# Unread transposes of W0 ahead of W1's on TensorE, a second pair of PSUM banks for one block's M, and a mask written by VectorE

## What is computed

```python
x = x + einsum('bct,bcd->bdt', x, W0[itok_B_0_7])      # x: 128 x 64 x 512 fp32, W0: 8 x 64 x 64
x = x + einsum('bct,bcd->bdt', x, W1[itok_B_1_198])    # W1: 200 x 64 x 64
```

## Time and profile before

| | us |
|---|---|
| Median of 3 runs | 93.66 (93.46, 93.66, 95.83) |
| Time of the profiled execution | 94.32 |
| Its span, first to last instruction | 92.5 (92.54 with two decimals) |
| What lies around the span | 1.8 |
| Busy: TensorE 72.8, VectorE 60.9, ScalarE 50.6, GpSimd 23.8 | |

### The profile page before, as it was taken

How to read it: one execution, slowest core, us unless ns; L and a number is a source line. 1 busy time by engine, 2 the same in 40 slices (tenths; PEclk the granted TensorE clock), 3 DMA queues, 4 the chain that set the end, 5 groups by cost and what they waited for, 6 DMA issues and landing times.

```text
span 92.5 us, 2284 instructions
## 1 busy us (share of the span) xinstructions
PE 72.8 (79%) x836; PEld 38.7 (42%) x836; DVE 60.9 (66%) x115; ACT 50.6 (55%) x95; POOL 23.8 (26%) x124
## 2 busy tenths in 40 slices
PE   0400009999299999999999999999999999999700
PEld 0200008899154545435445544754444444444200
DVE  0086003389527887888778788878788788787740
ACT  2300001468626776777567677677576676676630
POOL 4220009989999989000000000000000000000000
PEclk9999999999999999999999999999999999999995
DMA  0999999999999999999999999999999999879695
GB/s 16 330 457 390 430 395 420 413 411 405 416 405 404 400 411 404 409 407 416 398 411 413 418 409 418 420 409 420 420 421 418 414 418 416 361 310 388 276 402 228
DMA packets 9180, 35.92 MB, mean 388 GB/s; under 512 B 721, under 2 KB 850, under 8 KB 9042
## 3 DMA queue, kind: packets, MB, share of 16 engines
q1 hardware_dynamic: 8880, 33.56, 90.4%
q0 software_dynamic: 144, 2.10, 5.4%
q10 hardware_dynamic: 146, 0.13, 0.5%
HBM read 19.01 MB, written 16.78 MB: 387 GB/s over the span
## 4 chain that ended last, share of the span: by engine, by line
PE 73%; DMA 13%; DVE 6%; issue 2%; DVEq 1%; ACT 1%; POOLq 0%; ACTq 0%
PE psum L225 61%; DMA w_rows<-in_L_cond_weights_dram,cond 10%; PE psum L206 7%; PE psum L187 6%; DVE w L244 5%; DMA cond<-in_itok_B_dram 3%; DVEq L64 1%; DVE xy L266 1%; ACT m_diag L258 1%; DVE w_rows L306 0%; POOLq L160 0%; ACTq L250 0%; POOLq L151 0%
## 5 line engine op out<-in xcount | busy, mean ns | idle before, releaser
L225 PE MATMUL psum<-xy,m_diag 64*128 64x512 f32 x256 | 56.6, 594 | 0.0
L266 DVE COPY xy<-psum 64x512 f32<-64x512 f32 x64 | 43.7, 684 | 12.7 <-PE psum L225 11.7
L266 ACT COPY xy<-psum 64x512 f32<-64x512 f32 x64 | 37.2, 581 | 19.1 <-PE psum L225 18.3
L225 PEld LDWEIGHTS psum<-xy,m_diag 64*128 64x128 f32 x256 | 24.4, 187 | 27.7 <-issue 27.1
L168 POOL COPY w0b<-w0t 64x64 f32 x112 | 21.6, 235 | 10.3 <-DMA w_rows<-in_L_cond_weights_dram,cond 8.5
L187 PE MATMUL psum<-ident,w_rows 128*64 128x128 f32 x64 | 9.5, 323 | 9.3 <-DVE w_rows L306 9.3
L244 ACT COPY w<-psum 64x256 f32<-64x256 f32 x16 | 5.8, 364 | 15.3 <-PE psum L187 14.5
L187 PEld LDWEIGHTS psum<-ident,w_rows 128*64 128x64 f32 x64 | 8.4, 158 | 10.7 <-DVE w_rows L306 9.8
L244 DVE COPY w<-psum 64x256 f32<-64x256 f32 x16 | 6.7, 417 | 3.4 <-PE psum L187 3.0
L206 PE MATMUL psum<-w,w0b 64*32 64x64 f32 x512 | 6.5, 224 | 1.8 <-ACT m_diag L258 0.9
L258 DVE TENSOR_SCALAR m_diag<-psum,mask 128x256 f32<-128x256 f32 (+2 forms) x14 | 6.7, 517 | 1.9 <-PE psum L206 1.7
(11 more groups left out here) (6 smaller groups left out, 0.8 us busy)
## 6 DMA issues: line engine op xcount, KB each, us to landing
xy<-in_x_dram SPq DMA_DIRECT2D x15, 1024.0 KB, 19.5
out_dram<-xy SPq DMA_DIRECT2D x15, 1024.0 KB, 11.1
xy<-in_x_dram SPq DMA_DIRECT2D x2, 512.0 KB, 7.4
out_dram<-xy SPq DMA_DIRECT2D x2, 512.0 KB, 3.4
w_rows<-in_L_cond_weights_dram ACTq DMA_DIRECT2D x1, 128.0 KB, 2.6
cond<-in_itok_B_dram SPq DMA_DIRECT2D x1, 0.5 KB, 2.4
subjects<-in_itok_B_dram ACTq DMA_DIRECT2D x1, 0.5 KB
w_rows<-in_L_cond_weights_dram,cond POOLq DMA_INDIRECT x1, 9.5
```

The costliest lines, as they stand in the source:

```text
L225: last = nc.tensor.matmul(psum[:, 2 * (s % Y_RING) + h, :], m_diag[rows, odd, v % M_RING, j, :], xy[rows, s, j * T:(j + 1) * T], start=j = ...
L266: copy(xy[rows, s, i * T:(i + 1) * T], psum[HALVES[i], 2 * (s % Y_RING) + h, :]).then_inc(done, 1)
```

## The change

Three edits:

1. Behind the 4 transposes of W0, TensorE issues 52 more (`WARM`) of the same tiles of W0. They write `psum` banks 0 to 5, nobody reads them, they wait for nothing and raise no semaphore; W1's transposes overwrite those banks later.
2. `M_BANK` becomes a list, `M_BANKS`: block 1's M goes to banks 4 and 5, all others' stay in 6 and 7. products(1) has therefore no wait for the copies of block 0's M any more (`if k >= 2`).
3. The mask is written by VectorE, 8 memsets of 32 x 1 at the head of its program, in place of 5 memsets on GpSimd; the gather no longer waits for it. The waits on `s_mask` in `copies` go from 4 to 8.

```diff
-    M_BANK = 6
+
+    M_BANKS = [6, 4, 6, 6, 6, 6, 6]
...
+    WARM = 52
...
-            nc.gpsimd.memset(mask[:, :], 0.0).then_inc(s_zeros, 1)
-            pool.wait_ge(s_zeros, 2)
-            for r, rows in enumerate(QUARTERS):
-                nc.gpsimd.memset(mask[rows, r % 2:r % 2 + 1], 1.0).then_inc(s_mask, 1)
-            pool.wait_ge(s_mask, SLOT)
...
             last.then_inc(s_w0_turned, 1)
+            for n in range(WARM):
+                nc.tensor.transpose(psum[0:C, n % W1_RING, 0:P], w0_rows[:, n % ROWS, :], ident[:, :])
...
-                if k >= 1:
+                if k >= 2:
+
                     pe.wait_ge(s_m_v, 2 * k)
                     pe.wait_ge(s_m_s, 2 * k)
...
-                                last = nc.tensor.matmul(psum[QUARTERS[r], M_BANK + odd, at:at + C],
+                                last = nc.tensor.matmul(psum[QUARTERS[r], M_BANKS[k] + odd, at:at + C],
...
-                      psum[:, M_BANK + odd, at:at + n * J * C].rearrange("q (w e i) -> q w i e", i=J, e=Q),
+                      psum[:, M_BANKS[k] + odd, at:at + n * J * C].rearrange("q (w e i) -> q w i e", i=J, e=Q),
...
-            eng.wait_ge(s_mask, SLOT)
+            eng.wait_ge(s_mask, 2 * SLOT)
...
+            for r, rows in enumerate(QUARTERS):
+                for b in range(2):
+                    nc.vector.memset(mask[rows, b:b + 1], 1.0 if b == r % 2 else 0.0).then_inc(s_mask, 1)
+
```

## The result

The changed kernel takes 98.28 us, median of 4 runs (96.92 to 98.7), against 93.8 for the kernel before: the ratio is 1.041, 95% interval 1.025 to 1.057. It is slower, where the prediction said 1.2% faster. Some executions of any of these kernels take some per cent longer than the others; the times given are medians of all runs, and the ratios are taken without those. The profiled execution took 98.11 us, with a span of 96.1 in place of 92.5.

A forecast was written before the change was run, and what follows sets the result against it. TensorE's chain and DMA were taken as bounds side by side, DMA slack only in the tail. Gains of 2.25 and 0.46 us make 2.7 on TensorE, of which 1.1 arrives: 93.66 - 1.1 = 92.5 us, range 91.2 to 93.7.

The forecast's parts named there:

- Nothing else waits for them: At the head: the 52 added transposes lie wholly beside the wait for W1's gather and hold up nothing.
- Is anything late next?: Check of x's loads, GpSimd's copies and the last products: none would hold up TensorE's apply starting 2.7 us earlier.
- The late rival: Head: the 52 transposes stay slow, end at 15.4 and start W1's transposes 1.5 us late; 94.8 us, chance 0.05.
- Of the 1.6 us of pause that is left I assume that it leaves the pace high.: Between the added transposes' end at 12.3 and W1's at 13.88: TensorE's idle spell does not cost the fast pace.
- The pause rival: Ahead of W1's transposes: 1.6 us idle loses the high pace, the banks alone gain 0.46 us; 93.2 us, chance 0.08.
- The 2.25 us themselves: W1's transposes run fast from the start, so ScalarE's copies end at 21.9 in place of 24.15: gain 2.25 us.
- Transposes alone bring the higher pace.: W1's transposes, from 13.88: nothing else runs before the pace changes, so transposes raise it, against the skill's rule.
- holds nothing before its first change: Granted clock column during W1's transposes: its early 1.00 is not a reading; the pace there is taken as 1.2 GHz.
- The banks, 0.46 us.: products(1) runs directly behind products(0), beside the copies of M0, so apply(0) starts 0.46 us earlier; bounds 0 and 0.46.
- The mask, worth 0 within 0.1 either way.: Head: the gather never waited for GpSimd's mask memsets, so moving them gains 0; bounds 0.1 us loss or gain.
- Two bounds, of 2.7 us won 1.1 arrives.: Tail: TensorE ends 2.7 us earlier, but the full line of stores lets 1.1 us through; 1.6 us is not seen.
- The estimate of 91.4 for the span: Whole kernel, profiled execution: span 92.5 less the 1.1 us gain makes 91.4.

The follow-up runs named there:

- e1: The kernel before with 26 small unread matmul calls (104 TensorE instructions) behind W0's transposes and nothing else of the change: 97.52 us, ratio 1.034.
- e2: The changed kernel with 26 small unread matmul calls behind its 52 transposes, 208 TensorE instructions more than before: 93.27 us, ratio to before 0.991.
- e5: The kernel before with 13 small unread matmul calls behind W0's transposes (52 more TensorE instructions): 99.57 us, ratio 1.056.
- e9: The kernel before with 14 small unread matmul calls behind W0's transposes (56 more TensorE instructions): 98.25 us, ratio 1.044.
- e6: The changed kernel with its last two blocks of 4 units cut into four blocks of 2: 95.1 us, ratio 1.011.
- e7: The changed kernel with 26 small unread matmul calls behind its 52 transposes, and the mask left on GpSimd: 93.18 us, ratio 0.992.
- e10: As e6, the changed kernel with smaller last blocks, but with 66 unread transposes in place of 52: 93.44 us, ratio 0.993.
- e11: As e10, with 66 unread transposes and smaller last blocks, but the mask left on GpSimd: 93.47 us, ratio 0.992.
- e4: The kernel before with block 1's M in banks 4 and 5 and nothing else of the change: 94.38 us, ratio 1.000.
- e3: The kernel before with the mask set by VectorE and nothing else of the change: 94.39 us, ratio 1.006.
- e8: The changed kernel's mask and banks, with 52 matmul calls side by side in the array in place of the 52 unread transposes: 95.42 us, ratio 1.009.
- e12: The changed kernel with its own blocks and 26 calls side by side in the array, lasting 0.76 us, behind the transposes: 93.77 us, ratio 0.994.

## Why the prediction was wrong

- *"Nothing else waits for them"*, of the 52 transposes, and *"Is anything late next?"*. This is the step that failed. It went through x's loads, GpSimd's copies and the stores, and left out what TensorE consumes in every row: its own instructions. The sum had a term of 0 for them, and it measured 2.95 us. The last matmul was put at 84.8 and came at 91.04; of these 6.2 us the fetch is 2.95, W1's transposes, slow after all, 2.47 (2.25 not won, 0.22 lost), and their later start 0.82. e1 shows the loss with the count alone, e2 shows it gone with a larger count, e5 and e9 move it pair by pair, e6 takes away what it needs, and all six gaps of four kernels stand ahead of instruction 1217 or 1473. The late rival was on the right side but for another reason.
- *"Of the 1.6 us of pause that is left I assume that it leaves the pace high."* The assumption was named, with a chance of 0.08; it failed too, the second step to do so. The pause was 3.64 us: the transposes sped up sooner than after the 4.7 us of the execution before, ended at 11.05 and not at 12.3, and the gather came later. The 2.25 us were not there. The pace rival's own price (0.46 us of gain left) was of the right kind.
- *The 2.25 us themselves* were right. With the pause closed, e2 goes from W1's first transpose to the first product in 8.11 us and not 10.37: 2.26. e7, e10 and e11 take 8.11 too. That the difference comes out to the hundredth is luck: with a slow start the same stretch took 9.65 to 10.98 us from one execution to the next, a gain of 1.5 to 2.9.
- *Transposes alone bring the higher pace.* Right: 52 unread ones end 6.83 us after their start, where 211 ns each would make 11.0. The rule of the Trainium skill, "TensorE: Matmul & The Clock Gate", Part 4, that they don't is not borne out by any run here. The column of the granted clock, which read 1.00 in the earlier trace rows, reads 0.50 for the same pace in the changed kernel's trace: the reading "holds nothing before its first change" was right.
- *The banks, 0.46 us.* Right in place: 1.36 us in place of 1.86, in the changed kernel and in e4. In time e4 shows nothing of it (1.000, interval 0.996 to 1.005).
- *The mask, worth 0 within 0.1 either way.* Wrong in sign and size (e3: 0.5 us lost, interval 0.05 to 1.0). I took the gather's issue to be held by `cond` alone, as the memsets were over at 2.12. Yet without them it goes out at 3.38 to 3.57 in place of 3.98 to 4.12, and it lands at 14.03 to 14.79 in place of 13.50 to 13.89, e1 and e8 with their late landings left aside. Why a gather issued 0.6 us earlier lands 0.5 us later no run here tells; what changes with it is that SP, released by the gather's issue, sends x's next loads 0.7 us earlier too.
- *Two bounds, of 2.7 us won 1.1 arrives.* Right, where TensorE's gain was there at all. e2 ends TensorE at 85.34, 2.1 us before the kernel before, and has a span 1.0 us shorter and a ratio of 0.991; e7 and e11 end it at 85.76 and 85.66 with spans of 91.4 and 91.3. e10's profiled execution is the exception: TensorE ends 1.0 us before the kernel before, and the span is 92.3, only 0.2 shorter; its timed median is that of e11 all the same. The estimate of 91.4 for the span was met by the kernels in which the pause is closed and no gap stands. The versions that beat both kernels are e2, e7, e10, e11 and e12, by 0.6 to 0.9% against before: the tail's slack was 0.9 us, and none of them got much more than that.

## What to carry to other kernels

Instructions are something that an engine consumes, so work that "costs nothing" on an idle engine isn't free while the program behind it runs at 5.5 ns an instruction (256 in 1.4 us): look where runs of some 256 short instructions lie, and look for "issue" rows in the middle of a group whose operands are all there. When a change adds or removes instructions at the head and something slows far behind it, add a hundred idle ones more before explaining it otherwise; that costs one run. Warming up an engine must last until the work that it is meant for, and what it is worth is read from the bound that takes over, here the stores' line, not from the engine.

## What the runs showed of the hardware

- A packet of 16 KB on an instruction queue starts, and TensorE goes on 2.3 us later: 50.74 to 53.06 and 60.43 to 62.72 in the changed kernel, 52.34 to 54.65 and 62.02 to 64.31 in e1, 62.12 to 64.44 in e5; in e9 2.2 us, 60.63 to 62.84. In kernels without a gap the shortest distance from a packet's start to the border that it serves is 2.35 us (before), 2.41 (e3), 4.7 (e2). Why the packet starts when it does (at 60.43 in the changed kernel, though the piece before it was entered at 53.06) is open; it was not within a fixed number of instructions in these traces.
- The granted clock fell with pauses of 3.64 (the changed kernel), 2.10 (e6) and 2.33 us (e12, though not in each of its executions) ahead of W1's transposes, and not with 1.47 (e10) or none (e2, e7, e11). In the changed kernel it fell some 2 us into the pause, in e6 about 1 us into the work behind it.
- In e5 and e9, with a few small matmuls at the head, it fell in the midst of the pipeline's opening for over 3 us; the trace of the kernel before, with the same idle spells of 0.9 us, showed no such thing. Open.
